# A vision tower's first stage: half-integer angles about the middle of each part, the lower half read backwards

## The chip, the core and the metric

The kernel runs on one core of one Trainium2 chip. The core has a matrix engine (PE, with PEld for its weight loads), a vector engine (VectorE, DVE), a scalar engine (ScalarE, ACT), GpSimd (POOL) and a queue of DMA issues (SyncE, SP). The metric is device time in microseconds, from the launch of the program to its end, taken as the median of several executions.

## The reference, cut to what is computed

The first stage makes an S4D convolution kernel for 64 images `c` and 128 rows `h`:

```
dtA = (-exp(inv_A_real) + 1j * A_imag) * exp(log_dt)[:, None]        # 128 x 64
Cc  = (C[..., 0] + 1j*C[..., 1]) * (B[..., 0] + 1j*B[..., 1]) * (exp(dtA) - 1) / A
V   = exp(dtA[:, :, None] * arange(1024))
h   = 2 * einsum('chn,hnl->chl', Cc, V).real                         # 64 x 128 x 1024
h   = h + attention(layernorm(h));  h = h + ffn_with_lora(layernorm(h))
```

The attention and the feed-forward part run over 64 sequences of 128 tokens of width 1024; the change doesn't touch them.

## The kernel before

The program has three blocks with a barrier of all engines between them: the token stage (`token_kernel`), the preparation of the weights (`prepare_weights`), and the tower (attention and feed-forward, `turns`). The token stage writes its result to `tok_h` in device memory, and the tower reads it back.

**Splitting the length.** The 1024 positions are cut into `L1` = 4 parts of `L0` = 256. A position is part times 256 plus an offset, and exp(dtA * position) is exp(dtA * 256 * part) times exp(dtA * offset). The first factor goes into tables per part (`gre`, `gim`, built from `wmag`, `wre`, `wim` and the sines in `whole`), the second is made anew for each row h: `v` holds exp(re * offset) times the sine of the angle. Partitions are the 64 states n times two: even partitions have a quarter turn added (`C_Q`), so they hold the cosine, odd ones the sine.

**Chunks.** 128 rows h are worked in `NCH` = 16 chunks of `CH` = 8. `tabc` holds one chunk's columns of the tables: part tables for `z`, the rate for the exponential, the turns per step for the angle (row `NT - 1`). For each chunk:

- VectorE copies `tabc` (L395), computes for each of 8 rows the whole number of turns `k` (L399, offset times turns plus the quarter, written as an integer), and for each of 8 the fraction `u` (L404); 256 columns each.
- ScalarE makes `v` = exp (L292, eight of 256 columns) and the sine of `u` (L298, one of 2048 columns), in the order of `decay` and `sine`, which change places in every chunk, so that each chunk has one load of a function table.
- VectorE multiplies `v` by `u` (L411, one of 2048 columns).
- PE turns the input into `ct1`, `ct2` (L454); VectorE multiplies them by the part tables into `z` and `z2` (L419, L420); GpSimd adds the two (L244) and swaps pairs of the input into `xs` (L231).
- PE multiplies `z` by `v` into `kps` (L472): per row h two products, q = 0 and q = 1, each for two of the four parts.
- ScalarE copies `kps` to `kout` (L283), which has two halves of four rows; SP stores each half with two DMAs, e = 0 and 1 (L204).
- VectorE takes one sixteenth of the maximum of the raw weights (`part_max`, L426).

**The order of the work** is written out by hand and the same in every chunk. VectorE's `body(ch)` is: `tabc`, `k`, `u` of chunk ch + 1; `v` of chunk ch; `z`, `z2` of chunk ch + 1; `part_max`. GpSimd's sum of chunk ch waits for `z_parts` of ch and for `v_ready` of ch. PE's `kps` of chunk ch waits for that sum and for `v`. VectorE's `z` of chunk ch + 1 waits until GpSimd's sum of ch - 1 and PE's `kps` of ch - 1 are done, since `z` has two buffers (L417, L418). ScalarE's exponentials of chunk ch + 1 wait for the same `kps` (L290). A copy to the first row of a `kout` half waits for the stores of the chunk before (L282). SP's `body(ch)` is: two loads of the input of chunk ch + 3 (behind a wait for PE's transposes), two loads of the weight `wo`, and four stores of chunk ch - 1.

**Where the parts stand.** `out_v` (L146) reads the 1024 positions as (q e l): q and e pick the part, e is the half of the partitions and of a DMA. So a DMA writes, for each c and h, two runs of 256 numbers, 1 KB each, with 1 KB between them.

Of the kernel before, what the change touches and what calls it, by code (L numbers as in the profile page):

```python
# [7 lines left out]
P = 128  # L8
ALU = mybir.AluOpType
# [33 lines left out]
C_ONE = C_OWN + 1  # L43
C_ALL = C_ONE + 1


def constants():
# [13 lines left out]
    c[:, C_OWN] = np.arange(P) // R  # L61
    c[:, C_ONE] = 1
    return c


def token_kernel(nc, sem, x, log_dt, b_re_im, inv_a, a_imag, const, ident, w, tok_h):
# [3 lines left out]
    with ExitStack() as ctx:  # L70
# [12 lines left out]
        re = sb("re", [P, NS])  # L83
        turns = sb("turns", [P, 8, NS])
        whole = sb("whole", [P, 8, NS])
        sines = whole
        e0 = sb("e0", [P, NS])
        th = sb("th", [P, NS])
        wmag = sb("wmag", [P, L1 - 1, NS])
        wre = sb("wre", [P, L1 - 1, NS])  # L90
        wim = sb("wim", [P, L1 - 1, NS])
        gre = sb("gre", [P, L1, NS])
# [9 lines left out]
        xs = sb("xs", [P, 2, CH // 2, NS, 2])  # L102
        u = sb("u", [P, 2, CH, L0])
        k = sb("k", [P, CH, L0], I32)
        qb = sb("qb", [P, 1])
# [4 lines left out]
        tmp = spare[:, 0, 0:18 * NS].rearrange("p (i n) -> p i n", n=NS)  # L110
        mix = spare[:, 1, 0:18 * NS].rearrange("p (i m n) -> p i m n", i=6, n=NS)
        part_max = sb("part_max", [P, NCH])

# [141 lines left out]
        def _(act):  # L255
            def step(ins):
                ins.then_inc(s_at, 1)
# [6 lines left out]
            step(nc.scalar.activation(th[:, :], re[:, :], ACT.Tanh, scale=0.5))  # L264
            for m in range(1, L1):
                step(nc.scalar.activation(wmag[:, m - 1], re[:, :], ACT.Exp, scale=float(m * L0)))
            act.wait_ge(s_dt, 12)
            step(nc.scalar.activation(sines[:, :, :], turns[:, :, :], ACT.Sin, scale=TURN))
# [44 lines left out]
        def _(dve):  # L313
# [15 lines left out]
            step(TS(turns[:, 1], turns[:, 0], 0.5, None, ALU.mult))  # L329
            for m in range(1, L1):  # L330
                step(TS(turns[:, 2 * m], turns[:, 0], float(m * L0), None, ALU.mult))
                step(TS(turns[:, 2 * m + 1], turns[:, 0], float(m * L0), 0.25, ALU.mult, ALU.add))
            step(TS(tab_c[:, 0, NT - 1], turns[:, 0], 1.0, None, ALU.mult))
            TS(whole[:, :, :], turns[:, :, :], ROUND, -ROUND, ALU.add, ALU.add).then_inc(s_whole, 1)
            dve.wait_ge(s_whole, 1)
            step(TT(turns[:, :, :], turns[:, :, :], whole[:, :, :], ALU.subtract))
            dve.wait_ge(s_at, 8)
            t = [tmp[:, i] for i in range(18)]
# [23 lines left out]
            step(STT(t[1], t[16], 2.0, bi, ALU.mult, ALU.mult))  # L362
            step(TT(gre[:, 0], t[0], t[1], ALU.add))
            step(STT(t[2], t[15], 2.0, bi, ALU.mult, ALU.mult))
            step(STT(t[3], t[16], 2.0, br, ALU.mult, ALU.mult))
            step(TT(gim[:, 0], t[2], t[3], ALU.subtract))

            sc = sines[:, 2:2 * L1].rearrange("p (m a) n -> p a m n", a=2)
            step(TT(wim[:, :], wmag[:, :], sc[:, 0], ALU.mult))
            step(TT(wre[:, :], wmag[:, :], sc[:, 1], ALU.mult))  # L370
            g0r = gre[:, 0:1].to_broadcast([P, L1 - 1, NS])
            g0i = gim[:, 0:1].to_broadcast([P, L1 - 1, NS])
            step(TT(mix[:, 0], g0r, wre[:, :], ALU.mult))
            step(TT(mix[:, 1], g0i, wim[:, :], ALU.mult))
            step(TT(gre[:, 1:L1], mix[:, 0], mix[:, 1], ALU.subtract))
            step(TT(mix[:, 2], g0r, wim[:, :], ALU.mult))
            step(TT(mix[:, 3], g0i, wre[:, :], ALU.mult))
            step(TT(gim[:, 1:L1], mix[:, 2], mix[:, 3], ALU.add))

# [9 lines left out]
            def body(ch, r):  # L389
                nxt = 1 - r  # L390
                if exists(ch + 1):
                    if exists(ch - 1):

                        dve.wait_ge(s_e, ch)
                    V.tensor_copy(tabc[:, nxt], tab[:, :, bass.ds((ch + 1) * CH, CH)]).then_inc(s_tabc, 1)  # L395
                    dve.wait_ge(s_tabc, ch + 2)

                    for h in range(CH):
                        ins = TS(k[:, h], const[:, C_L0:C_L0 + L0], tabc[:, nxt, NT - 1, h:h + 1],  # L399
                                 const[:, C_Q:C_Q + 1], ALU.mult, ALU.add)  # L400
# [1220 lines left out]
```

## Time and profile before

| | us |
|---|---|
| median of three runs | 3096.68 |
| lowest and highest | 3093.18, 3097.64 |
| the profiled execution, its own time | 3095.41 |
| its span, first to last instruction | 3093.6 |
| token stage, to the barrier behind it | 268.8 |
| preparation of the weights and start of the tower, to 362 | 93.2 |
| the rest of the tower | 2731.6 |

Over the whole span PE is busy 2852.0 us (92%), VectorE 2500.3, GpSimd 1966.9, ScalarE 1913.8. Times in rows of the trace count from the first instruction. In a row of the stretches of time each engine has its busy time and the number of its instructions; `PEclk` is the granted clock of the matrix engine as a share of 2.4 GHz. In a row of the timeline the first two numbers are start and length in us, and the bracket at the end holds the idle time before and what ended it; a row with x8 is eight instructions from the start of the first to the end of the last, which overlap a little.

### The profile page before, as it was taken

How to read it: one execution, taken by the hardware profiler on the slowest of the kernel's cores; microseconds unless marked ns; L12 is line 12 of the kernel's file. 1: busy time of each engine (PE TensorE's matmuls, PEld its weight loads, DVE VectorE, ACT ScalarE, POOL GpSimd, SP SyncE). 2: the span in 40 equal slices, each digit the busy share in tenths (PEclk: the TensorE clock that was granted, in tenths of full speed). 3: DMA queues.
4: the chain of work that ended last, by engine and by line, in shares of the span. 5: the costliest groups of instructions: out<-in, count | busy, mean ns of one | idle time of the engine just before them, and what ended most of it. 6: DMA issues, size and time to landing. Idle time of an engine off the chain costs nothing.

```text
span 3093.6 us, 62128 instructions
## 1 busy us (share of the span) xinstructions
PE 2852.0 (92%) x16986; PEld 1418.5 (46%) x16986; DVE 2500.3 (81%) x8865; ACT 1913.8 (62%) x5932; POOL 1966.9 (64%) x1722
## 2 busy tenths in 40 slices
PE   3767469999999999999999999999999999999986
PEld 2556234444444444444444444444444444444442
DVE  8996568888888888888888888888888888888872
ACT  5775356666666666666666666666666666666651
POOL 2441157667777767676777676777776776777762
PEclk9887789999999999999999999999999999999998
DMA  5887166676666666766666666666666666666751
GB/s 160 190 182 176 33 125 142 141 150 148 148 143 146 147 148 141 152 147 147 144 146 148 148 141 152 148 148 143 146 145 147 143 150 146 150 142 149 140 125 52
DMA packets 1269008, 442.53 MB, mean 143 GB/s; under 512 B 1200048, under 2 KB 1241264, under 8 KB 1268800
## 3 DMA queue, kind: packets, MB, share of 16 engines
q1 hardware_dynamic: 1268800, 440.62, 65.2%
q14 instruction: 183, 1.50, 0.2%
q8 instruction: 25, 0.41, 0.1%
HBM read 88.15 MB, written 67.11 MB: 50 GB/s over the span
## 4 chain that ended last, share of the span: by engine, by line
PE 38%; DVE 19%; issue 13%; POOL 10%; ACT 7%; DMA 1%; DVEq 0%; ACTq 0%; POOLq 0%; SPq 0%
PE bank_b L1437 18%; PE bank_a L1437 13%; DVE heads L1258 6%; DVE probs L1204 5%; ACT probs L1079 5%; POOL p_hl L1004 4%; POOL probs L1000 3%; PE bank_c L1437 3%; PE score L1408 2%; POOL rope_a L1010 2%; DVE share L1213 2%; POOL xy_hl L1019 1%; PE pv L1426 1%; DVE r L1286 1%; DVE zs L1366 1%
## 5 line engine op out<-in xcount | busy, mean ns | idle before, releaser
L1079 ACT ACTIVATE probs<-probs,negmax 128x128 f32<-128x128 f32 x2048 | 789.7, 387 | 268.9 <-DVE negmax L1204 268.9
L1004 POOL TENSOR_TENSOR p_hl<-probs,p_hl 128x512 f16<-128x512 f32 x512 | 614.9, 1201 | 354.6 <-ACT p_hl L1088 352.3
L1000 POOL TENSOR_TENSOR probs<-probs,rsum 128x512 f32<-128x512 f32 x512 | 556.7, 1087 | 221.7 <-DVE rsum L1215 220.1
L1437 PE MATMUL bank_a<-qkv_hi,xt 128*128 128x512 f16 x2048 | 655.7, 382 | 28.9 <-DMA xt<-xy_hl 28.9
L1204 DVE CUSTOM_DVE_ANT_0 probs<-score,table,scal 128x128 f32<-128x128 f32 x2048 | 596.5, 347 | 58.2 <-issue 56.9
L1437 PE MATMUL bank_b<-b_hi,yt 128*128 128x512 f16 x2048 | 643.1, 381 | 0.0
L1088 ACT ACTIVATE p_hl<-probs 128x512 f16<-128x512 f32 x512 | 319.8, 625 | 424.7 <-POOL probs L1000 417.2
L1258 DVE TENSOR_TENSOR heads<-rope_a,heads 128x512 f16<-128x512 f32 x320 | 402.4, 1273 | 36.5 <-ACT heads L1109 36.5
L1437 PE MATMUL bank_a<-qkv_lo,xt 128*128 128x512 f16 x1024 | 390.7, 381 | 0.0
L1437 PE MATMUL bank_b<-b_lo,yt 128*128 128x512 f16 x1024 | 390.0, 381 | 0.0
L1437 PE MATMUL bank_b<-o_lo,at_hi 128*128 128x512 f16 x1024 | 388.9, 380 | 0.0
L1437 PE MATMUL bank_b<-o_hi,at_hi 128*128 128x512 f16 x1024 | 388.8, 380 | 0.0
L1437 PE MATMUL bank_b<-o_hi,at_lo 128*128 128x512 f16 x1024 | 388.7, 380 | 0.0
L1079 ACT ACTIVATION_READ_ACCUMULATOR probs<-probs,negmax 128x1 f32 x2048 | 382.9, 187 | 0.0
L1109 ACT ACTIVATE heads<-rope_a 128x512 f16<-128x512 f32 x320 | 192.7, 621 | 246.8 <-POOL rope_a L1010 241.5
L1437 PE MATMUL bank_c<-qkv_hi,xt 128*128 128x512 f16 x1024 | 325.9, 380 | 0.0
L1437 PEld LDWEIGHTS bank_a<-qkv_hi,xt 128*128 128x128 f16 x2048 | 201.3, 98 | 271.7 <-issue 32.4
L1437 PEld LDWEIGHTS bank_b<-b_hi,yt 128*128 128x128 f16 x2048 | 201.0, 98 | 222.2 <-issue 4.6
L1019 POOL TENSOR_TENSOR xy_hl<-xyn,xy_hl 128x1024 f16<-128x1024 f32 x128 | 273.0, 2133 | 30.6 <-ACT xyn L1121 25.6
L1213 DVE TENSOR_TENSOR share<-sums,small 128x4 f32<-128x4 f32 x512 | 198.3, 387 | 72.0 <-ACT probs L1079 53.0
L1010 POOL TENSOR_TENSOR rope_a<-rope_a,rope_b 128x512 f32<-128x512 f32 (+1 forms) x192 | 208.9, 1088 | 36.8 <-DVE rope_b L1241 34.0
L1408 PE MATMUL score<-kstack,stack 128*128 128x128 f16 x2048 | 198.5, 220 | 24.9 <-DVE negmax L1204 17.9
(199 smaller groups left out, 4525.2 us busy)
## 6 DMA issues: line engine op xcount, KB each, us to landing
tok_h<-kout SPq DMA_DIRECT2D x64, 512.0 KB, 5.9
hin<-tok_h SPq DMA_DIRECT2D x64, 512.0 KB, 3.3
r<-tok_h SPq DMA_DIRECT2D x64, 512.0 KB, 3.5
out_dram<-r SPq DMA_DIRECT2D x64, 512.0 KB, 2.9
probs_t<-p_hl SPq DMA_TRANSPOSE x512, 2.8
xc<-in_x_dram SPq DMA_DIRECT2D x32, 128.0 KB, 4.7
raw_a<-in_L_attn_wq_dram SPq DMA_DIRECT2D x1, 4096.0 KB, 14.4
raw_b<-in_L_attn_wo_dram SPq DMA_DIRECT2D x32, 128.0 KB, 3.8
```

Of the source, the lines that this page charges most:

```text
L1000: TT(x, x, rsum[:, u % 4].unsqueeze(2).to_broadcast([P, GR, T]), ALU.mult).then_inc(s_norm, 1)
L1004: TT(p_hl[:, u % 2, 1], probs[:, u % 4], p_hl[:, u % 2, 0], ALU.subtract).then_inc(s_plo, 1)
L1010: TT(rope_a[:, 0:hs], rope_a[:, 0:hs], rope_b[:, 0:hs], ALU.add).then_inc(s_rope2, 1)
L1019: TT(xy_hl[:, 1], xyn[:, :], xy_hl[:, 0], ALU.subtract).then_inc(done, 1)
L1079: ins = A(probs[:, u % 4, g], probs[:, u % 4, g], ACT.Exp, bias=negmax[:, u % 4, g:g + 1], scale=-1.0, accum_out=sums[:, u % 4, g:g + 1])
L1088: A(p_hl[:, u % 2, 0], probs[:, u % 4], ACT.Copy).then_inc(s_phi, 1)
L1109: A(dst, src, ACT.Copy).then_inc(s_hhi, 1)
L1204: ins = V.tensor_tensor_reduce(probs[:, u % 4, g], score[u % 2][:, g], mask, col(U_SC), 3e38, ALU.add, ALU.min, negmax[:, u % 4, g:g + 1])
L1213: TT(share[:, u % 4], sums[:, u % 4], small[:, :], ALU.mult).then_inc(s_share, 1)
L1258: TT(dst, full_.unsqueeze(2).to_broadcast([P, 8, 2, HD]), hi, ALU.subtract).then_inc(s_hlo, 1)
L1408: ins = MM(score[u % 2][:, g], stack[:, h // 8, h % 8], kstack[:, par, u], start=True, stop=True)
L1437: ins = MM(bank, x(c), w[:, c, cols], start=(c == 0 and i == 0), stop=(c == KC - 1 and i == 2))
```

## The change

The offset inside a part is taken about the middle of the part. The part tables now belong to the position 256 * part + 127.5, for all four parts (before, part 0 had no factor of its own); so there are four pairs of sines instead of three, and `wmag`, `wre`, `wim` have four rows. The offsets of a part are then -127.5 to 127.5, and the angle of a negative offset is that of the positive one with the sign turned. `k`, `u` and the sine are made for the 128 positive half-integer offsets alone. The cosine is even and the sine odd: the upper half of `v` is multiplied by `u` as it stands, the lower half by `u` read backwards (a step of -1) times `C_SIGN`, +1 on even partitions and -1 on odd ones. The exponential is still taken for 256 columns, from offset 0 on; its part factor remains that of the start of the part.

`PART` = (0, 2, 1, 3) gives the order of the parts in the tables, and `out_v` reads the positions as (e q l). The products q = 0 and q = 1 of one half of the partitions are now neighbouring parts, and a DMA writes one run of 512 numbers, 2 KB, for each c and h.

```diff
+PART = (0, 2, 1, 3)
+LH = L0 // 2
...
+    c[0::2, C_SIGN] = 1
+    c[1::2, C_SIGN] = -1
+    c[:, C_HALF:C_HALF + L0 // 2] = np.arange(L0 // 2)[None, :] + 0.5
...
-        u = sb("u", [P, 2, CH, L0])
-        k = sb("k", [P, CH, L0], I32)
+        u = sb("u", [P, 2, CH, LH])
+        k = sb("k", [P, CH, LH], I32)
...
-        out_v = tok_h.rearrange("c h (q e l) -> e c h q l", e=2, l=L0)
+        out_v = tok_h.rearrange("c h (e q l) -> e c h q l", e=2, l=L0)
...
-            for m in range(1, L1):
-                step(nc.scalar.activation(wmag[:, m - 1], re[:, :], ACT.Exp, scale=float(m * L0)))
+            for i in range(L1):
+                step(nc.scalar.activation(wmag[:, i], re[:, :], ACT.Exp, scale=float(PART[i] * L0)))
...
-            for m in range(1, L1):
-                step(TS(turns[:, 2 * m], turns[:, 0], float(m * L0), None, ALU.mult))
-                step(TS(turns[:, 2 * m + 1], turns[:, 0], float(m * L0), 0.25, ALU.mult, ALU.add))
+            for i in range(L1):
+                middle = PART[i] * L0 + LH - 0.5
+                step(TS(turns[:, 2 * i + 2], turns[:, 0], middle, None, ALU.mult))
+                step(TS(turns[:, 2 * i + 3], turns[:, 0], middle, 0.25, ALU.mult, ALU.add))
...
-                        ins = TS(k[:, h], const[:, C_L0:C_L0 + L0], tabc[:, nxt, NT - 1, h:h + 1],
+                        ins = TS(k[:, h], const[:, C_HALF:C_HALF + LH], tabc[:, nxt, NT - 1, h:h + 1],
...
-                        ins = STT(u[:, nxt, h], const[:, C_L0:C_L0 + L0], tabc[:, nxt, NT - 1, h:h + 1], k[:, h],
+                        ins = STT(u[:, nxt, h], const[:, C_HALF:C_HALF + LH], tabc[:, nxt, NT - 1, h:h + 1], k[:, h],
...
-                    TT(v[:, r], v[:, r], u[:, r], ALU.mult).then_inc(s_v, 1)
+                    upper, lower = v[:, r, :, LH:L0], v[:, r, :, 0:LH]
+                    TT(upper, upper, u[:, r], ALU.mult)
+                    STT(lower, u[:, r, :, ::-1], const[:, C_SIGN:C_SIGN + 1], lower, ALU.mult, ALU.mult).then_inc(s_v, 1)
```

The remaining lines of the diff widen the tables: `turns` and `whole` from 8 to 10 rows, the products of the table step from 192 to 256 columns, the result for the first position in a place of its own (`g0`), and the constants by 129 columns.

On VectorE, one chunk near the start of the program (its `tabc` to its `part_max`), first in the kernel before:

```order
L395 COPY tabc<-tab 128x80
L399 TENSOR_SCALAR k<-const,tabc 128x256 x8
L404 SCALAR_TENSOR_TENSOR u<-const,tabc,k 128x256 x8
L411 TENSOR_TENSOR v<-v,u 128x2048
L419 TENSOR_TENSOR z<-ct,tabc 128x2048
L420 TENSOR_TENSOR z<-ct,tabc 128x2048
L426 TENSOR_REDUCE part_max<-raw_a 128x1
```

and the same chunk on VectorE in the changed kernel:

```order
L404 COPY tabc<-tab 128x80
L408 TENSOR_SCALAR k<-const,tabc 128x128 x8
L413 SCALAR_TENSOR_TENSOR u<-const,tabc,k 128x128 x8
L421 TENSOR_TENSOR v<-v,u 128x8x128
L422 SCALAR_TENSOR_TENSOR v<-u,const,v 128x8x128
L430 TENSOR_TENSOR z<-ct,tabc 128x2048
L431 TENSOR_TENSOR z<-ct,tabc 128x2048
L437 TENSOR_REDUCE part_max<-raw_a 128x1
```

Nothing changes its place; `k` and `u` have half their columns, and the one product for `v` became two, of which the second releases GpSimd and PE.

On GpSimd, the sums and swaps of the first chunks of the changed kernel, which stand as before:

```order
L239 TENSOR_TENSOR xs<-xc,const 128x256 x6
L252 TENSOR_TENSOR z<-z 128x2048
L239 TENSOR_TENSOR xs<-xc,const 128x256 x2
L252 TENSOR_TENSOR z<-z 128x2048
L239 TENSOR_TENSOR xs<-xc,const 128x256 x2
```

The sum of `z` still stands right behind the wait for `v`, with one swap of the input between two sums.

## Rows read from the trace of the kernel before

**Rows 1.** Stretches of time: length, then busy time of each engine.

```profile
43.39:239.64 196.25, 133.53 (x543) 110.90 (x544) 191.59 (x296) 151.54 (x248) 78.39 (x40) 0.88 0.76 172
239.64:268.78 29.14, 18.42 (x75) 14.68 (x73) 10.95 (x8) 17.39 (x30) 9.43 (x4) 0.92 0.82 193
```

The engines stand in the order PE, PEld, DVE, ACT, POOL; behind them the granted clock, the DMA share and GB/s.

**Rows 2.** Groups of VectorE between 43.3 and 239.6 us: busy us, mean ns.

```profile
L404 DVE SCALAR_TENSOR_TENSOR u<-const,tabc,k 128x256 f32<-128x256 f32 x113 | 46.1, 479 | 0.5
L399 DVE TENSOR_SCALAR k<-const,tabc 128x256 int32<-128x256 f32 x112 | 38.7, 417 | 0.5
...
L411 DVE TENSOR_TENSOR v<-v,u 128x2048 f32<-128x2048 f32 x14 | 32.0, 2284 | 0.0
```

**Rows 3.** Waits between 43 and 248 us: total, times, longest.

```profile
DVE z L419 <- PE kps L472: 3.6, 4, 1.4
```

**Rows 4.** Timeline, chunks 0 to 2 and the `v` of chunk 14.

```profile
43.39 2.28 DVE L411 TENSOR_TENSOR v<-v,u 128x2048 f32<-128x2048 f32 x1
45.59 2.28 DVE L419 TENSOR_TENSOR z<-ct,tabc 128x2048 f32<-128x2048 f32 x1
45.82 4.52 POOL L244 TENSOR_TENSOR z<-z 128x2048 f32<-128x2048 f32 x1 [12.38 <-DVE v L411]
...
50.39 9.93 PE L472 MATMUL kps<-v,z 128*128 128x256 f32 x32 [10.95 <-POOL z L244]
...
57.13 2.28 DVE L411 TENSOR_TENSOR v<-v,u 128x2048 f32<-128x2048 f32 x1
...
60.46 2.29 DVE L419 TENSOR_TENSOR z<-ct,tabc 128x2048 f32<-128x2048 f32 x1 [1.05 <-PE kps L472]
...
65.45 2.00 ACT L298 ACTIVATE u<-u,qb 128x2048 f32<-128x2048 f32 x1
...
65.95 2.67 DVE L399 TENSOR_SCALAR k<-const,tabc 128x256 int32<-128x256 f32 x8
68.66 3.26 DVE L404 SCALAR_TENSOR_TENSOR u<-const,tabc,k 128x256 f32<-128x256 f32 x8
71.84 2.28 DVE L411 TENSOR_TENSOR v<-v,u 128x2048 f32<-128x2048 f32 x1
...
239.64 2.28 DVE L411 TENSOR_TENSOR v<-v,u 128x2048 f32<-128x2048 f32 x1
```

**Rows 5.** PE's `kps`: timeline of chunks 1 and 2, stretches of chunks 1 and 10.

```profile
64.14 7.57 PE L472 MATMUL kps<-v,z 128*128 128x256 f32 x32 [2.95 <-POOL z L244]
...
78.93 5.44 PE L472 MATMUL kps<-v,z 128*128 128x256 f32 x14 [6.34 <-POOL z L244]
...
191.29 7.08 PE L472 MATMUL kps<-v,z 128*128 128x256 f32 x21 [6.34 <-POOL z L244]
...
64.14:71.71 7.57, 7.44 (x34) 6.21 (x35) 7.50 (x19) 5.23 (x7) 1.09 (x2) 1.00 0.90 224
191.29:200.75 9.46, 9.46 (x34) 7.95 (x35) 8.87 (x19) 5.77 (x11) 1.41 (x3) 0.75 0.76 161
```

**Rows 6.** Groups of VectorE before 26 us, the table step.

```profile
L332 DVE TENSOR_SCALAR turns<-turns 128x64 f32<-128x64 f32 x3 | 0.6, 195 | 0.1
L341 DVE SCALAR_TENSOR_TENSOR z<-whole 128x64 f32<-128x64 f32 x1 | 0.2, 226 | 0.8 <-ACT whole L268 0.8
...
L361 DVE SCALAR_TENSOR_TENSOR z<-z,bri x1: 226/226/226, 15.9 to 15.9; 128x64 f32<-128x64 f32 x1
```

**Rows 7.** Timeline of ScalarE's last copies, behind the fifteenth `v`.

```profile
259.98 2.06 ACT L283 ACTIVATE kout<-kps 128x512 f32<-128x512 f32 x4 [3.85 <-DMA tok_h<-kout]
264.21 2.07 ACT L283 ACTIVATE kout<-kps 128x512 f32<-128x512 f32 x4 [2.16 <-DMA tok_h<-kout]
```

**Rows 8.** One instruction's ns (least, median, most), and two stretches of time.

```profile
L1258 DVE TENSOR_TENSOR heads<-rope_a,heads x320: 661/853/2859, 372.8 to 2989.9; 128x512 f16<-128x512 f32 x160
...
10.00:20.00 10.00, 0.00 (x0) 0.00 (x0) 8.23 (x31) 0.63 (x1) 0.86 (x1) 1.00 1.02 412
131.00:134.00 3.00, 0.00 (x0) 0.00 (x0) 3.00 (x2) 2.97 (x6) 3.00 (x1) 1.00 0.93 221
```

More of the change, by code:

```diff
@@ L43 @@
 C_ONE = C_OWN + 1
-C_ALL = C_ONE + 1
+C_SIGN = C_ONE + 1
+C_HALF = C_SIGN + 1
+C_ALL = C_HALF + L0 // 2
 def constants():
@@ L83, in token_kernel @@
         re = sb("re", [P, NS])
-        turns = sb("turns", [P, 8, NS])
-        whole = sb("whole", [P, 8, NS])
+        turns = sb("turns", [P, 2 + 2 * L1, NS])
+        whole = sb("whole", [P, 2 + 2 * L1, NS])
         sines = whole
@@ L88, in token_kernel @@
         th = sb("th", [P, NS])
-        wmag = sb("wmag", [P, L1 - 1, NS])
-        wre = sb("wre", [P, L1 - 1, NS])
-        wim = sb("wim", [P, L1 - 1, NS])
+        wmag = sb("wmag", [P, L1, NS])
+        wre = sb("wre", [P, L1, NS])
+        wim = sb("wim", [P, L1, NS])
+        g0 = sb("g0", [P, 2, NS])
         gre = sb("gre", [P, L1, NS])
@@ L110, in token_kernel @@
         tmp = spare[:, 0, 0:18 * NS].rearrange("p (i n) -> p i n", n=NS)
-        mix = spare[:, 1, 0:18 * NS].rearrange("p (i m n) -> p i m n", i=6, n=NS)
+        mix = spare[:, 1, 0:6 * L1 * NS].rearrange("p (i m n) -> p i m n", i=6, n=NS)
         part_max = sb("part_max", [P, NCH])
@@ L264, in _ @@
             step(nc.scalar.activation(th[:, :], re[:, :], ACT.Tanh, scale=0.5))
-            for m in range(1, L1):
-                step(nc.scalar.activation(wmag[:, m - 1], re[:, :], ACT.Exp, scale=float(m * L0)))
-            act.wait_ge(s_dt, 12)
+            for i in range(L1):
+                step(nc.scalar.activation(wmag[:, i], re[:, :], ACT.Exp, scale=float(PART[i] * L0)))
+            act.wait_ge(s_dt, 14)
             step(nc.scalar.activation(sines[:, :, :], turns[:, :, :], ACT.Sin, scale=TURN))
@@ L336, in _ @@
             step(TT(turns[:, :, :], turns[:, :, :], whole[:, :, :], ALU.subtract))
-            dve.wait_ge(s_at, 8)
+            dve.wait_ge(s_at, 9)
             t = [tmp[:, i] for i in range(18)]
@@ L362, in _ @@
             step(STT(t[1], t[16], 2.0, bi, ALU.mult, ALU.mult))
-            step(TT(gre[:, 0], t[0], t[1], ALU.add))
+            step(TT(g0[:, 0], t[0], t[1], ALU.add))
             step(STT(t[2], t[15], 2.0, bi, ALU.mult, ALU.mult))
             step(STT(t[3], t[16], 2.0, br, ALU.mult, ALU.mult))
-            step(TT(gim[:, 0], t[2], t[3], ALU.subtract))
-            sc = sines[:, 2:2 * L1].rearrange("p (m a) n -> p a m n", a=2)
+            step(TT(g0[:, 1], t[2], t[3], ALU.subtract))
+            sc = sines[:, 2:2 * L1 + 2].rearrange("p (m a) n -> p a m n", a=2)
             step(TT(wim[:, :], wmag[:, :], sc[:, 0], ALU.mult))
             step(TT(wre[:, :], wmag[:, :], sc[:, 1], ALU.mult))
-            g0r = gre[:, 0:1].to_broadcast([P, L1 - 1, NS])
-            g0i = gim[:, 0:1].to_broadcast([P, L1 - 1, NS])
+            g0r = g0[:, 0:1].to_broadcast([P, L1, NS])
+            g0i = g0[:, 1:2].to_broadcast([P, L1, NS])
             step(TT(mix[:, 0], g0r, wre[:, :], ALU.mult))
             step(TT(mix[:, 1], g0i, wim[:, :], ALU.mult))
-            step(TT(gre[:, 1:L1], mix[:, 0], mix[:, 1], ALU.subtract))
+            step(TT(gre[:, :], mix[:, 0], mix[:, 1], ALU.subtract))
             step(TT(mix[:, 2], g0r, wim[:, :], ALU.mult))
             step(TT(mix[:, 3], g0i, wre[:, :], ALU.mult))
-            step(TT(gim[:, 1:L1], mix[:, 2], mix[:, 3], ALU.add))
+            step(TT(gim[:, :], mix[:, 2], mix[:, 3], ALU.add))
             step(V.tensor_copy(tab_c[:, 0, 0:L1], gre[:, :]))
```

## The prediction

> **What bounds the kernel now.** The first look is at where the changed stage lies. By the stretches of time, the first stage with its sixteen chunks ends at 268.78 us; between the first `v` product (43.39 us) and the fifteenth (239.64 us) VectorE is busy 191.6 of 196.25 us, PE 133.5, ScalarE 151.5, GpSimd 78.4 [rows 1]. Read by that alone, the stage is VectorE's, and every VectorE microsecond taken away comes back. The groups of instructions say how it is spent: per chunk 8 instructions for `k`, 8 for `u`, one for `v`, two for `z`, one for `part_max` [rows 2].
>
> The waits say something finer. VectorE's own waits are only 3.6 us, but all of them are its `z` product waiting for PE's `kps` [rows 3]. That wait closes a loop over two chunks: the `v` product of chunk c releases GpSimd's sum of `z`; that releases the `kps` matmuls of chunk c; their end frees the `z` buffer for chunk c+2; behind that, on VectorE, stand `z`, `z2`, `part_max`, `tabc`, `k` and `u` of chunk c+2, and then a `v`. From the rows of chunk 0: `v` starts at 43.39, GpSimd at 45.82 (2.43 later), PE at 50.39 (4.57), `z` at 60.46 (PE 9.93 and 0.14 more), the `v` of chunk 2 at 71.84 (11.38). The sum is 28.45 us for two chunks: with no slack anywhere [rows 4]. Over the seven such pairs the mean is (239.64 - 43.39)/7 = 28.04 us [rows 4]. VectorE alone, without the wait, takes 13.74 us from the `v` of chunk 0 to that of chunk 1 [rows 4], 27.5 us a pair. So loop and engine lie 2% apart, and the question is what each loses.
>
> **The change part by part.**
>
> `k` and `u`, 128 instead of 256 columns, 8 of each a chunk. 2048 columns of `v` take 2284 ns and the next instruction starts 2.20 us after it; 64 columns take 226 ns [rows 2, 4, 6]: (2284 - 226)/1984 = 1.04 ns a column. So each of the 16 loses 128 x 1.04 = 0.133 us. `k` to `u` is 2.71 us now (65.95 to 68.66), `u` to `v` 3.18 us [rows 4]; they become 1.64 and 2.11. **2.13 us less a chunk.**
>
> `v`, one product of 2048 columns, becomes a product of 1024 columns and a second instruction of 1024 columns that reads `u` backwards. The columns are the same in number. The extra start is 2.20 - 2048 x 1.04 = 0.07 us [rows 2, 4]; instructions of the second kind cost some more to start (`u`: 479 ns for 256 columns, against 417 for `k` [rows 2]), 0.06 us. **0.13 us more a chunk**, on VectorE as well as in the loop, if the backward read costs what a forward one does. No row shows a backward read. From below, nothing excludes a saving but nothing can give one either, for both forms already run at one column each 1.04 ns. From above, the slowest two-input product of this kernel is the `heads` one, 2859 ns for 512 columns beside 661 at best [rows 8], that is 5.6 ns a column: 4.6 us more a chunk. The nearest row is a strided read: `bri` is read with a step of two, and takes 226 ns for 64 columns, as do the products of the same size with step one [rows 6]. I take no extra cost, and keep the upper end for a rival.
>
> The Trainium skill speaks against this. "Vector Engine (DVE) Microarchitecture Reference", section 5.2 on the measured stream behaviour, says that a port runs at its full rate only where successive elements come as adjacent pairs of words, and gives 1.73 ns a column where one source hops at every element; it adds that a negative step was not measured. By that figure the estimate is 0.7 us more for a chunk's backward half. The step-two read above does not bear the rule out, since 64 columns would be 0.04 us slower by it.
>
> `Sin` on 1024 instead of 2048 columns takes about 1 us off ScalarE. ScalarE is busy 151.5 us in 196.25 [rows 1] and is not what the loop passes through. Behind the end of chunk 0's `kps` (60.32) its copy, the exponentials, a table load and the sine of chunk 2 are through at 67.45, 7.1 us later [rows 4]; that becomes 6.1, while the `v` that needs them follows `kps` by 0.14 + 9.25. So nothing is won there, and some 3 us of cover are left.
>
> **The loop after.** v to GpSimd 2.43 + 0.12, GpSimd to PE 4.57, PE as now, `z` to `v` 11.38 - 2.13. The loop holds only one chunk's worth of `k` and `u` for its two chunks, so it loses 2.0 us, not the 4.0 that VectorE loses: 28.04 - 2.0 = 26.0 us a pair. VectorE alone would need 2 x (13.74 - 2.0) = 23.5. The `z` wait takes the place of what was removed: about 2.5 us a pair, all of it before every second chunk, since the odd chunk follows the even one at VectorE's pace, 11.7 us later. Seven pairs: **14.0 us less** between the two `v`.
>
> PE's term rests on its clock. `kps` took 7.57 us at a granted clock of 1.00 (2.4 GHz) behind an idle stretch of 2.95 us, and 9.46 us with a granted clock of 0.75 on average (part at 1.2 GHz) behind one of 6.34 us [rows 5]. In the new schedule the odd chunk's `kps` starts 11.7 us after the even one's, PE stands idle about 1.5 us (11.7 less 9.3 and 0.9 of transposes, 71.71 to 72.59 [rows 5]) and should stay at 2.4 GHz; but that chunk's loop has slack. The even chunk's starts 14.3 us after the odd one's, which takes 7.6, and the transposes 0.9: idle 5.8 us, so it should start at 1.2 GHz as it does now. The loop that decides keeps its slow PE.
>
> **Before the first `v`.** `k` and `u` of chunks 0 and 1 lose 2 x 2.13 = 4.3 us. The tables grow: two more steps of 0.2, eight products of 256 instead of 192 columns (8 x 64 x 1.04 = 0.53 us), the two over 640 instead of 512 columns and the sine of the same size 0.13 each [rows 6], and 66 KB more of constants before the first step, 0.2 to 0.3 us at 412 to 221 GB/s [rows 8], if nothing hides it. Together 1.5 us more. **2.8 us less.**
>
> **Behind the fifteenth `v`.** 29.1 us now [rows 1]. `kps` of chunk 14 follows as before. The last copies wait for stores: 3.85 and 2.16 us [rows 7]. The stores' runs become 2 KB. Loads in 4 KB runs moved 412 GB/s at a full DMA share, the mix with stores in 1 KB runs 221 GB/s at 0.93 [rows 8]. A store pair of 1 MB that took 4.2 us (259.98 to 264.21 [rows 7]) then takes 3.3 or so. Two pairs: 1.7 us less, between 0 and 3.5. Between the two `v` no copy waits for a store, so the longer runs win nothing there.
>
> **The sum:** 14.0 + 2.8 + 1.7 = 18.5 us less. What follows the stage starts at its end and depends on nothing that has an earlier fixed time, so it moves as a whole. The profiled execution is 3095.41 us, 3093.6 of them span; it lies 1.3 us under the median of three, 3096.68. From it 3076.9; from the median 3078.2. I give 3077.5.
>
> **The rivals.**
>
> *PE keeps 2.4 GHz in both chunks.* Then `kps` takes 7.6 instead of 9.3 us in the deciding loop, 1.7 a pair, 12 us in all: 3065. For it: gaps of 2.95 us kept the clock. Against: the gap before even chunks should be 5.8. Chance 0.12.
>
> *The stage is VectorE's after all,* because PE's wait disappears in some way that I don't see: seven pairs of 23.5, 32 + 4.5 us less: 3060. The loop above adds up to 0.01 us, so 0.03.
>
> *The backward read runs at half speed,* 1.07 us more for each of 15 chunks. Both `v` and VectorE carry it, but the even loop holds it once a pair, so 7 or 8 times 1.07: 8 to 9 us of the gain are gone, 3086. This is the rival that the skill's rule of adjacent pairs gives, at its price somewhat less. Chance 0.15.
>
> *Slower than before:* the backward read costs so much that it eats everything. 18.5 us over 8 is 2.3 us a chunk, 3.3 ns a column; from there on it is slower. At the 5.6 ns of the slowest product, 4.6 us a chunk, VectorE takes over with 2 x (11.7 + 4.6) = 32.6 a pair, 4.6 more than now, and once more behind the fifteenth: 3095.4 + 32 + 5 - 4.5 = 3128. Chance 0.04. That the half-size instructions hit a floor and save nothing is the same to the reader and nearly excluded: 64 columns run in 195 to 226 ns.
>
> **How the numbers follow.** The forecast has 0.66, and its own range is 3072 to 3083 (table cost, tail 0 to 3.5 us, PE's term up to 0.5 us a pair either way). The range goes down to the clock rival and up to the slow read: 3063 to 3088. About 0.2% (6 us) is what a measurement of this kernel can tell from no change; only a backward read at 2.5 to 4 ns a column ends there, which I take out of the slow read's chance. Faster 0.91, same 0.05, slower 0.04.
>
> **What would show it.** In the profile after: `k` near 280 ns and `u` near 345 ns; the second `v` instruction near 1.28 us (a slow read shows there, at once); the wait of `z` for `kps` grown from 3.6 us to 15 or 20 us; `v` starts alternating at 11.7 and 14.3 us; PE's granted clock falling only before even chunks; ScalarE's two waits for `kout` stores near the end shortened. It is wrong if ScalarE's `v` exponentials or the stores' landing become a wait before `v` or `kps`.

## The result and the profile after

| us | before | after |
|---|---|---|
| median, lowest and highest | 3096.47 (3093.18 to 3097.64) | 3116.56 (3115.38 to 3118.36) |
| the profiled execution, its span | 3095.41, 3093.6 | 3116.39, 3114.6 |
| first `v` product | 43.39 | 40.86 |
| `v` product of chunk 14 | 239.64 | 230.88 |
| end of the token stage | 268.78 | 258.93 |
| tower's first scores on VectorE | 389.10 | 381.30 |
| tower's last scores on VectorE | 3022.7 | 3043.6 |

The changed kernel is slower: the ratio is 1.0066, with an interval of 1.005 to 1.0082. I had forecast 3077.5 and given "slower" a chance of 0.04. One execution below, of the kernel without GpSimd's wait, took 3496.0 us at a granted clock of 0.83 instead of 0.96, and no ratio counts it. The table splits the miss in two. The token stage gained 9.9 us where 18.5 were forecast, and the tower, in which no line of code was changed, lost 28.7 (the preparation between them took 2.1 more).

The stretches of time, columns as in [rows 1]; first the stage (against [rows 1]), then preparation and tower of after:

```profile
40.86:230.88 190.02, 133.13 (x550) 109.84 (x551) 170.23 (x310) 138.16 (x248) 78.44 (x40) 0.89 0.77 179
230.88:258.93 28.05, 16.35 (x67) 13.21 (x66) 11.13 (x10) 16.58 (x30) 9.43 (x4) 0.86 0.83 198
258.93:381.30 122.37, 71.87 (x348) 53.13 (x348) 74.62 (x119) 47.82 (x71) 10.66 (x14) 0.71 0.33 81
381.30:3043.60 2662.30, 2581.62 (x15752) 1216.02 (x15753) 2176.79 (x8312) 1673.96 (x5538) 1849.06 (x1644) 0.99 0.67 143
```

The same stretches of before, which the earlier sections didn't need:

```profile
268.78:389.10 120.32, 70.37 (x348) 52.70 (x348) 74.60 (x119) 48.17 (x72) 10.66 (x14) 0.71 0.33 83
389.10:3022.70 2633.60, 2578.53 (x15752) 1214.73 (x15753) 2175.11 (x8312) 1673.26 (x5538) 1849.94 (x1644) 0.99 0.67 145
```

In the tower each engine runs the same instructions, PE at the same clock, and each is busy as long as before to 3.1 us. So the 28.7 us are idle time. VectorE's waits between 700 and 2700 us that end on "issue" (in total, times, longest), of before:

```profile
DVE probs L1204 <- issue: 25.7, 51, 0.7
DVE share L1213 <- issue: 13.2, 24, 0.9
```

and of after, where `L1215` is the old `L1204`:

```profile
DVE stats L1272 <- issue: 38.9, 24, 2.1
DVE probs L1215 <- issue: 17.1, 24, 0.7
```

24 times, once in each pass of VectorE's loop in this stretch, VectorE stands still for 1.6 us ahead of `stats`, and no semaphore holds it: "issue" is time for which the profile shows no wait. PE feels it a little later. Its waits in the same stretch grow from 14.9 us to 36.7 in all; before, and then after:

```profile
PE pv L1541 <- DVE zs L1366: 14.9, 24, 1.1
```

```profile
PE pv L1552 <- DVE zs L1377: 28.7, 24, 1.2
PE pv L1437 <- DMA probs_t<-p_hl: 6.6, 11, 1.0
PE pv L1437 <- issue: 1.4, 8, 0.3
```

The place is just behind the loop's jump. One pass on the timeline of VectorE, before. The jump is no row: in the program it stands between the first two rows, and VectorE's sequencer takes it at 796.93, while the engine still works off what was issued ahead of it:

```profile
797.97 0.74 DVE L1293 SCALAR_TENSOR_TENSOR r<-bank_c,scal,r 128x512 f32<-128x512 f32 x1
799.85 0.75 DVE L1278 SCALAR_TENSOR_TENSOR r<-bank_b,scal,r 128x512 f32<-128x512 f32 x1 [1.14 <-PE bank_b L1437]
800.64 0.69 DVE L1261 BATCH_NORM_STATS2 stats<-r 128x6 f32<-128x512 f32 x1
```

and after (the jump at 792.42):

```profile
793.46 0.74 DVE L1304 SCALAR_TENSOR_TENSOR r<-bank_c,scal,r 128x512 f32<-128x512 f32 x1
795.43 0.75 DVE L1289 SCALAR_TENSOR_TENSOR r<-bank_b,scal,r 128x512 f32<-128x512 f32 x1 [1.23 <-PE bank_b L1448]
797.98 0.69 DVE L1272 BATCH_NORM_STATS2 stats<-r 128x6 f32<-128x512 f32 x1 [1.80 <-issue]
```

Each kernel stops once at the jump. The bracket names PE, but by the records of VectorE's sequencer the first instruction behind the jump comes 2.8 us after it before and 2.9 after, and the product follows 0.14 us later. After has a second stop one product further on. A pass of two sequences takes 82.44 us before and 83.54 after (median of 27); 28 passes by 1.1 us are 31.

The stops go with the arrival of code. The page of after has this row (packets, MB, share) among its DMA queues:

```profile
q14 instruction: 183, 1.50, 0.2%
```

1.50 MB in 183 packets are 8.2 KB each. Five of them come back in every pass: by the records of the packets they start 1.0, 3.6, 6.7, 32.5 and 61.6 us behind the jump before, and 1.0, 3.5, 6.6, 33.7 and 59.4 after (medians over the passes). So the body of the loop is fetched anew in every pass. That VectorE waits for it behind the jump is read from these times: in the pass shown of after, the first two loads have landed 1.75 and 4.2 us behind the jump, and the two stops end at 2.9 and 5.6. In the compiled program VectorE's loop has 379 instructions. In front of it stand 954 before and 964 after: two more steps of the tables, and the second `v` instruction, written out in eight places. By the figures of the Trainium skill, "Runtime: NRT & Kernel Launch", section "Instruction fetch mechanics", 256 instructions are 16 KiB, 64 bytes each, and 16 KiB is a block. The loads of this queue are half as large, and the measurement decides: by 64 bytes each, one holds 128 instructions. The place of the loop's start in such a block moves from 58 to 68 (954 and 964 less whole 128s). It is counted as if a block began with the program's first instruction; that isn't shown, and only the distance between two kernels, modulo 128, is used here. The same section warns that a taken branch whose target isn't loaded stalls the engine until it is; the rows here agree. That the place matters, not only the jump, had to be tried.

### The profile page after: what moved, and what is told of

Same layout as the page of the kernel before. It is cut to its first block, busy times and chain, and to the rows that moved or that the text cites. A ratio compares the mean times of both kernels' runs of the same rounds, so it can differ in the third digit from the quotient of the medians.

```text
span 3114.6 us, 62147 instructions
## 1 busy us (share of the span) xinstructions
PE 2854.2 (92%) x16986; PEld 1417.7 (46%) x16986; DVE 2478.4 (80%) x8883; ACT 1899.3 (61%) x5933; POOL 1966.1 (63%) x1722
## 4 chain that ended last, share of the span: by engine, by line
PE 39%; DVE 18%; issue 13%; POOL 10%; ACT 7%; DMA 2%; DVEq 0%; ACTq 0%; POOLq 0%; SPq 0%
PE bank_b L1448 20%; PE bank_a L1448 12%; DVE heads L1269 6%; DVE probs L1215 5%; ACT probs L1090 5%; POOL p_hl L1015 4%; POOL probs L1011 3%; PE bank_c L1448 2%; PE score L1419 2%; DVE share L1224 2%; POOL rope_a L1021 1%; PE pv L1437 1%; POOL xy_hl L1030 1%; DVE r L1297 1%; DVE zs L1377 1%
## 5 line engine op out<-in xcount | busy, mean ns | idle before, releaser
L1215 DVE CUSTOM_DVE_ANT_0 probs<-score,table,scal 128x128 f32<-128x128 f32 x2048 | 598.7, 348 | 50.0 <-issue 49.3
L1024 POOL TENSOR_TENSOR rstd<-var,minus_half 128x1 f32<-128x1 f32 x128 | 70.8, 553 | 264.4 <-DVE var L1281 231.5
```

The costliest lines, as they stand in the source:

```text
L1024: TT(rstd[:, :], var[:, :], minus_half[:, :], ALU.pow).then_inc(done, 1)
L1215: ins = V.tensor_tensor_reduce(probs[:, u % 4, g], score[u % 2][:, g], mask, col(U_SC), 3e38, ALU.add, ALU.min, negmax[:, u % 4, g:g + 1])
```

## The experiments

Eleven more kernels ran, in three sets: the first four below, the next four, and the last three, of which the kernel before without its loop is one. Each is compared with the kernel before as run beside its set (medians 3100.72, 3095.74 and 3099.62). In the first set, theory C says that the place of VectorE's code makes the loss, and its rival that the wider constants do, which move the tiles behind them in memory.

**Ten idle instructions in the kernel before.** Behind the last chunk VectorE waits for the barrier; there it now fills ten single columns of a tile that nobody reads.

```diff
+        fill = sb("fill", [P, 128])
...
             V.tensor_reduce(w["mx"][:, 0:1], part_max[:, :], AX_X, ALU.max).then_inc(w["s_mx"], 1)
+            for i in range(10):
+                V.memset(fill[:, i:i + 1], 0.0)
```

> The kernel before, with 10 one-column fills more on VectorE where it stands idle for 17 us at the end of the first stage. 10 is the number of VectorE instructions by which the change makes the program longer ahead of the tower's loop. Theory C (the code's place): in the changed kernel VectorE stands still twice behind the loop's jump, once for 1.8 us where nothing else is due, since the loop's first instructions lie otherwise in the blocks in which code is loaded; so these 10 idle fills alone cost what the change cost in the tower, 25 to 30 us, and the kernel takes 3120 to 3127. Theory M (memory): the tower is slower since constants or the stored result lie otherwise in memory; then 10 fills cost nothing, 3096.

Measured: 3129.54 us, a ratio of 1.0094 (1.0077 to 1.0111). The fills themselves cost 0.19 us inside an idle stretch, by VectorE's timeline:

```profile
250.51 0.19 DVE L435 MEMSET fill<- 128x1 f32 x10
268.38 0.15 DVE L639 TENSOR_SCALAR mxa<-mxa 128x1 f32<-128x1 f32 x1 [17.68 <-PEq L70]
```

The stretch of the tower and VectorE's wait in it are those of after:

```profile
388.70:3055.70 2667.00, 2581.72 (x15752) 1216.02 (x15753) 2176.06 (x8312) 1673.73 (x5538) 1849.73 (x1644) 0.99 0.67 143
```

```profile
DVE stats L1264 <- issue: 42.8, 24, 2.1
```

So ten instructions that do nothing, ahead of the tower, cost 29 us. The kernel before, without one line of the change in it, shows the whole loss. The new tile `fill` isn't the cause: the kernels with 118 and with 16 fills below have the same tile, and their towers take 2634.8 and 2647.5 us.

**The wider constants alone.**

```diff
-C_ALL = C_ONE + 1
+C_ALL = C_ONE + 1 + 129
```

> The kernel before with the 129 further columns of constants and nothing else: every tile and every array in device memory behind it moves as in the changed kernel, VectorE's code stays. Theory M: 3115 to 3125. Theory C: 3096 to 3097 (0.2 us for the longer load).

Measured: 3099.27 us, 0.9997 (0.9988 to 1.0007). The rival falls.

**The changed kernel with 118 fills**, so that 10 + 118 = 128 instructions stand ahead and the loop has its old place in a block.

```diff
+            for i in range(118):
+                V.memset(fill[:, i:i + 1], 0.0)
```

> The changed kernel with 118 fills more on VectorE in its 16.6 us of idle time before the barrier: with the 10 of the change a whole block of 128 instructions (8 KB), so the tower's loop lies in its block as in the kernel before. Theory C: the 29 us of the tower come back, and what is left is the first stage's gain of 9.9 us less some 2 us of the weights' preparation: 3086 to 3090. Theory M: 3116.

Measured: 3089.05 us, 0.9958 (0.9941 to 0.9975). The second stop is gone, and PE's wait has its old length:

```profile
383.10:3017.90 2634.80, 2580.00 (x15752) 1214.52 (x15753) 2175.46 (x8312) 1673.72 (x5538) 1849.93 (x1644) 0.99 0.67 145
```

```profile
PE pv L1555 <- DVE zs L1380: 15.6, 24, 1.2
```

Pushing the loop to the same place brings the tower back to 2634.8 us against 2633.6, and what the change is worth by itself comes out: 11.7 us by the medians, 0.4%, with an interval of some 8 to 18 us. The traces say less: the two profiled executions differ by 4.6 us (3095.41 and 3090.78). The change also lengthens ScalarE's code by one instruction ahead of its loop. That is still so here, so it costs nothing that shows.

**Sixteen fills** put the loop's start at 84 in its block.

```diff
+            for i in range(16):
+                V.memset(fill[:, i:i + 1], 0.0)
```

> The changed kernel with 16 fills more: the block's edge, which now lies some 8 instructions behind the loop's entry, comes to lie before it. Theory C: one stall a pass instead of two; 3080 to 3092, unless the edge falls on another wait. Theory M: 3116.

Measured: 3101.54 us, 1.0005 (0.9995 to 1.0014), above what I expected. There is one stop again, but a longer one, up to 2.7 us:

```profile
DVE r L1292 <- issue: 51.9, 24, 2.7
```

The loads come 0.5, 1.0 and 4.3 us behind the jump here. I had taken one stop as good as another, and had put the edge of a block some 8 instructions behind the loop's entry, where the count above has 60. That the place costs something in three sizes is shown (table below); a rule that gives the size from the place I don't have.

**Stores in runs of 1 KB again**, with the 118 fills.

```diff
-PART = (0, 2, 1, 3)
+PART = (0, 1, 2, 3)
...
-        out_v = tok_h.rearrange("c h (e q l) -> e c h q l", e=2, l=L0)
+        out_v = tok_h.rearrange("c h (q e l) -> e c h q l", e=2, l=L0)
```

> The changed kernel with 118 fills, and with the order of the parts and of the stores as before (two runs of 1 KB instead of one of 2 KB). Against the same with 2 KB runs (3089.0). Theory of the prediction: the longer runs are worth only the last copies' waits for stores; those were 3.85 and 2.16 us and are 3.29 and 1.77 in the changed kernel, so this is 0.5 to 2 us slower, 3089.5 to 3091, and the wait behind the fifteenth v grows by that. Rival (the stores' landing became a wait in the faster stage, or the tower gains from the order of the parts): 5 us or more slower.

Measured: 3085.93 us, 0.9971 (0.996 to 0.9982), where I had expected 3089.5 to 3091; the interval overlaps that of the 2 KB runs (0.9941 to 0.9975). ScalarE's waits for the stores behind chunk 14, with 1 KB and then with 2 KB:

```profile
ACT kout L292 <- DMA tok_h<-kout: 5.7, 2, 3.6
```

```profile
ACT kout L292 <- DMA tok_h<-kout: 5.0, 2, 3.3
```

So the longer runs are worth 0.7 us of waiting in these two traces, less than the times can tell.

**GpSimd's sum no longer waits for `v`**, 118 fills. If the loop of two chunks is what sets the pace, cutting its first link should speed it up.

```diff
-                    pool.wait_ge(s_v, ch + 1)
```

> The changed kernel with 118 fills, where GpSimd's sum of z no longer waits for v (it doesn't read v; PE waits for both anyway). Theory L (the loop through GpSimd and PE is what holds the stage): v releases PE directly, the loop of two chunks loses some 4.6 us, VectorE's wait for kps (18.8 us in the changed kernel) vanishes, and a pair of chunks goes from 27.15 to 24.5 us: 17 to 19 us less, 3070 to 3073. Rival P (the sum now runs beside VectorE's own reads): GpSimd's 4.5 us fall on part_max, k and u; u, which reads two tiles, takes up to twice as long, and a part or all of the gain is gone: 3075 to 3095, u's mean well over 345 ns.

Measured: 3126.68 us, 1.0098 (1.0078 to 1.0118), worse than either account had it; a pair of chunks takes 32.5 us (mean of the first seven), where the kernel with 118 fills has 27.3. GpSimd starts right behind `z2`, and VectorE's copy of `tabc` runs into it. From the timeline in the middle of the stage:

```profile
151.53 4.53 POOL L252 TENSOR_TENSOR z<-z 128x2048 f32<-128x2048 f32 x1 [10.65 <-DVE z L431]
152.22 3.90 DVE L404 COPY tabc<-tab 128x80 f32 x1
```

The copy takes 0.19 us in after and 3.9 here, and ends when the sum does (156.06 and 156.12). `part_max` (0.95 us) runs beside the sum unharmed. Two copies a pair at 3.7 us more, on top of VectorE's own 24.6 (twice the 12.28 us from one `v` to the next, where it doesn't wait), would make 32.0: nearly the whole pair. So the wait that I took for a mere link of the loop also keeps GpSimd away from the copy.

**The loop away.** Now VectorE's loop of the tower is changed, and that of no other engine; 118 fills with the first edit, none with the others.

```diff
-        def turns(eng, turn):
+        def turns(eng, turn, step=2):
...
-            with eng.Fori(2, CB // 2 - 2) as pair:
-                turn(pair * 2, 0, True, True, True, True, True)
-                turn(pair * 2 + 1, 1, True, True, True, True, True)
+            if step:
+                with eng.Fori(4 // step, (CB - 4) // step) as some_:
+                    for i in range(step):
+                        turn(some_ * step + i if i else some_ * step, i % 2, True, True, True, True, True)
+            else:
+                for b in range(4, CB - 4):
+                    at(turn, b)
...
-            turns(dve, turn)
+            turns(dve, turn, 4)
```

> The changed kernel with 118 fills, and VectorE's loop of the tower written out for four turns a pass instead of two (same work, 14 jumps instead of 28; the other engines keep their loops). Theory C: a jump costs 1.4 us of standstill that shows, and the delay behind it; half of them gone is 14 x 1.4 to 14 x 2 us: 3061 to 3070. If the standstill has cover elsewhere: 3085 to 3090.

Measured with four sequences in a pass, half as many jumps: 3075.61 us, 0.9938 (0.9921 to 0.9954). And with VectorE's part written out, in the changed kernel and in the kernel before, by the same edit with another last line:

```diff
-            turns(dve, turn)
+            turns(dve, turn, 0)
```

> The changed kernel without fills, VectorE's part of the tower written out wholly, so that it has no jump there and its code comes in order. Theory C: no standstill behind a jump, and the place of the code doesn't matter any more: 28 x 1.4 to 28 x 2 us less than 3089, 3033 to 3050. Rival: code that is never used twice has to be loaded all along (about 80 blocks more), and the loads become waits of their own: 3070 or more.

> The kernel before with VectorE's part of the tower written out wholly, no loop, as in a_flat. Between this and a_flat nothing is left of the code's place, so the pair gives what the change is worth by itself. Theory C: a_flat less the first stage's 9.9 us: the profiled executions differ by 8 to 11 us, this one at 3073 to 3078 where a_flat has 3065 to 3067; the runs' ratio to the kernel before is near 0.993 (a_flat: 0.990). If the change slows the tower in another way too, the two come out alike.

Measured: 3065.29 us, 0.9898 (0.9881 to 0.9915), for the changed kernel, and 3072.57 us, 0.9916 (0.9899 to 0.9932), for the kernel before. The tower of the former:

```profile
383.00:2994.00 2611.00, 2573.94 (x15752) 1217.29 (x15753) 2142.04 (x8314) 1673.48 (x5538) 1848.75 (x1644) 0.99 0.66 146
```

So in the kernel before the loop costs 23 us of the tower and 27 of the whole, 0.8%. I had expected more (3061 to 3070 with four sequences a pass, 3033 to 3050 written out): a jump costs 0.9 us of the tower in both (2634.8 less 2621.7 over 14 jumps, 2634.8 less 2610.9 over 28), not the 1.4 to 2 that I took. The packets bear out whose code it is: the queue `q14` has 155 of them with four sequences a pass and 115 with VectorE's part written out. Between the two kernels without a loop the ratios differ by 0.0018, 5.6 us, and the profiled executions by 5.1 (3072.14 and 3067.03), below the 8 to 11 that I had expected; the intervals of the two ratios overlap.

With its part written out, VectorE is also busy some 33 us less in the tower (2142 against 2175), which I didn't follow up.

All towers in one table, sorted by the place of the loop's start in a block of 128 (counted as above); the time is from the first to the last scores on VectorE, read from each trace:

| place | tower, us |
|---|---|
| 58 | before 2633.6, wider constants 2637.3, 118 fills 2634.8, 1 KB runs 2633.2, GpSimd without its wait 2634.2 |
| 68 | after 2662.3, ten fills 2667.0 |
| 84 | sixteen fills 2647.5 |
| four sequences a pass | 2621.7 |
| no loop | 2610.9, 2610.6 (before), 2610.0, 2609.1 |

Inside a row the traces agree within 5 us, from row to row they differ by at least 10.

**`tabc` and `k` in other forms**, loop written out. The copy becomes a product with a column of ones, `k` an instruction with two tile inputs, to see whether it is the copy's form that runs into GpSimd.

```diff
-                    V.tensor_copy(tabc[:, nxt], tab[:, :, bass.ds((ch + 1) * CH, CH)]).then_inc(s_tabc, 1)
+                    TT(tabc[:, nxt], tab[:, :, bass.ds((ch + 1) * CH, CH)],
+                       const[:, C_ONE:C_ONE + 1].unsqueeze(1).to_broadcast([P, NT, CH]), ALU.mult).then_inc(s_tabc, 1)
...
-                        ins = TS(k[:, h], const[:, C_HALF:C_HALF + LH], tabc[:, nxt, NT - 1, h:h + 1],
-                                 const[:, C_Q:C_Q + 1], ALU.mult, ALU.add)
+                        ins = STT(k[:, h], const[:, C_HALF:C_HALF + LH], tabc[:, nxt, NT - 1, h:h + 1],
+                                  const[:, C_Q:C_Q + 1].to_broadcast([P, LH]), ALU.mult, ALU.add)
```

> a_flat, with two VectorE instructions of the first stage in another form, the results the same: tabc by a product with a column of ones instead of a copy, k by the form with two tile inputs (u's form). Reason: k lost only 0.52 ns a column when it was halved (407 to 340 ns), u 1.04, so k and the copy read one tile through two ports. Theory R (that form needs the port that GpSimd uses, and waits for GpSimd): k rises or falls by under 10 ns in the middle, but its 520 ns maxima and tabc's 0.56 and 0.66 us ones beside GpSimd's swap are gone; the stage is held by the loop, so its length changes by under 2 us.

Measured: 3063.67 us (3063.17 to 3065.05), 0.9886 (0.9869 to 0.9902). That can't be told from the kernel without this edit (0.9898), but lies 8.9 us under the kernel before without its loop, which ran beside it (3072.14 to 3074.42). It is the fastest kernel here. The long instructions that I had expected to vanish are still there: `k` reaches 585 ns (520 before the edit) and `tabc` 540.

The same with GpSimd's wait taken out:

```diff
-                    pool.wait_ge(s_v, ch + 1)
```

> a_oneport, and GpSimd's sum doesn't wait for v, as in a_free. In a_free the copy of tabc took 3.89 instead of 0.2 us, since it waited for GpSimd's sum to end, and the pair of chunks rose to 32.7 us. Theory R: with no instruction in the two-port form between z2 and v, the sum of GpSimd runs beside part_max, tabc, k and u, and only VectorE's own time is left: a pair near 2 x 12.2 = 24.5 us, the stage 17 to 19 us shorter than in a_flat, 3045 to 3050. Theory P (any VectorE instruction with two tile inputs loses beside GpSimd): k and u rise, to as much as twice, a pair stays at 27 us or more, 3065 or more.

Measured: 3105.07 us, 1.0018 (1.0009 to 1.0028), a pair 32.8 us. The account that only the copy's form collides falls: the product stands still as long as the copy did. `k` and `u` keep their medians (339 and 346 ns), since the sum is over when they start.

```profile
152.91 4.52 POOL L251 TENSOR_TENSOR z<-z 128x2048 f32<-128x2048 f32 x1 [10.76 <-DVE z L431]
153.60 3.93 DVE L403 TENSOR_TENSOR tabc<-tab,const 128x80 f32<-128x80 f32 x1
```

The Trainium skill, "SBUF — State Buffer", section "Who interferes with whom", lists both: a copy in its fast mode and any VectorE instruction with two inputs in SBUF block against a GpSimd instruction that reads SBUF. The rows agree. `z` and `z2`, with one input in PSUM, keep their 2.28 us beside the sum.

## Why the prediction was wrong

**The step that failed** is the sentence under the sum: "What follows the stage starts at its end and depends on nothing that has an earlier fixed time, so it moves as a whole." It is true of the data and of the semaphores, and for those I had looked. It isn't true of the code: ten instructions more on VectorE shift everything behind them in the program, and a loop that is fetched anew in each of 28 passes meets that shift 28 times. Shown by the kernel before with ten fills (+29 us) and the changed kernel with 118 (the loss gone). The chance for "slower" had the wrong mechanism too: it put the loss into the backward read. There were rows to be looked at: [rows 1] ends with the first stage, and no group holds VectorE's waits of the tower, where "issue" ends 24 waits of `share`, one in each pass. Such a wait, once a pass, is a mark of the loop.

**The stage, term by term.** Of 18.5 us it gave 9.85 in the profiled pair. Over the four traces with the stage of before its end lies between 266.3 and 268.8, over five with the changed stage between 258.9 and 260.9; the means differ by 7.6. The groups of after that answer to [rows 2] (least, median, most ns of one):

```profile
L408 DVE TENSOR_SCALAR k<-const,tabc x128: 332/340/520, 27.7 to 228.4; 128x128 int32<-128x128 f32 x128
L413 DVE SCALAR_TENSOR_TENSOR u<-const,tabc,k x128: 342/345/352, 29.8 to 230.6; 128x128 f32<-128x128 f32 x128
L421 DVE TENSOR_TENSOR v<-v,u x16: 1214/1217/1227, 40.9 to 238.7; 128x1024 f32<-128x1024 f32 x16
L422 DVE SCALAR_TENSOR_TENSOR v<-u,const,v x16: 1275/1279/1283, 42.0 to 239.9; 128x1024 f32<-128x1024 f32 x16
```

- *Backward read:* right. 1279 ns for 1024 columns, forecast 1.28 us; a forward product of the same size takes 1217, and 60 of the 62 ns between them were forecast for the form. That the 60 fit is luck: they were `u` less `k` at 256 columns, and `k` runs at half the price a column (next point). At 128 columns the two differ by 5 ns. The price that I had taken from the rule of adjacent pairs, 0.7 us more a chunk, isn't there, and the rival built on it is gone. The columns of a backward read are neighbours too, so the rule itself isn't tested by it.
- *`u`:* right, 345 ns as forecast.
- *`k`:* wrong by half. From 407 to 340 ns for 128 columns less is 0.52 ns a column, where I took 1.04 from the two-input products. `k` has one tile input and another form; its own rate wasn't in the rows that I used, since all `k` were of one size. The Trainium skill has a reason for it: by "VectorE: DVE Perf Modes", section "Mode 2×_2P", an instruction with a single tile input, in SBUF, reads it through both ports, two numbers at a time, and one with two tile inputs can't. The measured slopes agree; no run changed the number of tile inputs at 256 columns. Worth 8 x 128 x 0.52 = 0.53 us a chunk, 3.7 in the seven pairs.
- *The loop:* its form was right, its length wasn't. `z` waits for `kps` 18.8 us in all (forecast 15 to 20, against [rows 3]), and the `v` starts alternate at 12.3 and 14.9 us (forecast 11.7 and 14.3). The wait, then one loop from chunk 4 to chunk 6 on the timeline, against [rows 4]:

```profile
DVE z L430 <- PE kps L483: 18.8, 7, 2.8
```

```profile
94.64 1.22 DVE L421 TENSOR_TENSOR v<-v,u 128x1024 f32<-128x1024 f32 x1
...
97.20 4.52 POOL L252 TENSOR_TENSOR z<-z 128x2048 f32<-128x2048 f32 x1 [9.11 <-DVE v L422]
...
101.85 10.05 PE L483 MATMUL kps<-v,z 128*128 128x256 f32 x32 [5.72 <-POOL z L252]
...
106.92 1.21 DVE L421 TENSOR_TENSOR v<-v,u 128x1024 f32<-128x1024 f32 x1
...
112.04 2.29 DVE L430 TENSOR_TENSOR z<-ct,tabc 128x2048 f32<-128x2048 f32 x1 [2.71 <-PE kps L483]
...
121.82 1.22 DVE L421 TENSOR_TENSOR v<-v,u 128x1024 f32<-128x1024 f32 x1
```

  2.56 + 4.65 + 10.05 + 0.14 + 9.78 = 27.18 us; the mean of the seven is 27.15, forecast 26.0, before 28.04.
- *PE's term:* mis-sized. The even chunks' `kps` take 10.05 us on average over the seven pairs, before 9.34; I had let them stay. That is 0.71 us a pair, 5 us in all. With `k` it makes 26.0 + 0.53 + 0.71 = 27.24, against the 27.15 measured. The stretches of one even and one odd `kps` of after, against [rows 5]:

```profile
101.86:111.90 10.04, 10.04 (x34) 8.35 (x35) 7.39 (x20) 4.79 (x9) 3.46 (x3) 0.71 0.66 134
114.00:122.00 8.00, 7.00 (x31) 5.90 (x32) 7.93 (x21) 6.16 (x12) 1.14 (x2) 1.00 0.94 241
```

  Before, three even chunks, 4, 8 and 12:

```profile
106.86:115.71 8.85, 8.85 (x34) 7.43 (x35) 8.78 (x19) 5.77 (x11) 1.04 (x2) 0.81 0.85 172
162.49:172.69 10.20, 10.20 (x34) 8.43 (x35) 8.88 (x19) 5.78 (x12) 2.15 (x3) 0.70 0.74 150
219.26:228.12 8.86, 8.86 (x34) 7.48 (x35) 8.79 (x19) 5.76 (x12) 1.13 (x2) 0.81 0.73 147
```

  and on PE's timeline one even chunk of before; then one of after, with the odd one behind it (its first half of 16):

```profile
106.86 8.86 PE L472 MATMUL kps<-v,z 128*128 128x256 f32 x32 [4.46 <-POOL z L244]
```

```profile
129.03 10.12 PE L483 MATMUL kps<-v,z 128*128 128x256 f32 x32 [5.71 <-POOL z L252]
...
141.31 3.72 PE L483 MATMUL kps<-v,z 128*128 128x256 f32 x16 [1.29 <-POOL z L252]
```

  PE's idle stretches came out as forecast, 5.7 us (5.8) ahead of even and 1.2 to 1.7 us (1.5) ahead of odd chunks. The granted clock is 0.71 on average in the one and 1.00 in the other, so the rival that PE keeps its clock in both is out. What failed is the price. Before, three of the six even chunks behind the first had 0.81 and took 8.8 to 8.9 us, and three had 0.70 to 0.76 and took 9.3 to 10.2; after, all six have 0.70 to 0.72 and take 9.9 to 10.2. The mean that I kept was that of the mixture. The length of the idle stretch alone doesn't decide it: before, chunks 2 and 10 stood behind 6.34 us, longer than any of the six of after, and took 9.3 and 9.5, while chunk 8 stood behind 4.48 and took 10.2. Why the new rhythm gives every even chunk the long form stays open; no run changed PE's idle time alone.
- *Before the first `v`:* 2.53 us, forecast 2.8.
- *Behind the fifteenth:* 1.09 us (29.14 to 28.05), forecast 1.7. ScalarE's two waits for the stores went from 3.85 + 2.16 [rows 7] to 5.1 us. The kernel with runs of 1 KB (5.7 against 5.0 us, above) gives the longer runs 0.7 of that, which the times can't tell from nothing.

```profile
ACT kout L291 <- DMA tok_h<-kout: 5.1, 2, 3.3
```

Preparation and start of the tower took 122.4 us, before 120.3. Over all traces here it is 119.3 to 122.4, with the change and without, so I read nothing from it.

The signs of the steps were right, then, and their sum about twice too large: the price of `k` (3.7 us) and PE's term (5.0) account for the 8.7 that are missing. Neither decided the case. With the loop back in its place the changed kernel is faster than before by some 5 to 12 us, 0.2 to 0.4%, by whichever pair of kernels one takes, and the stage's own 7.6 lies in that; what the prediction left out, 29 us, is more than twice the most of it.

## What to carry to other kernels

Where an engine runs a loop, an edit anywhere ahead of it in that engine's code can move the time, by 1% here, without a semaphore or an instruction that explains it: count the instructions that an edit adds ahead of each loop, look for "issue" waits that come once a pass, and compare two versions only with the loop at the same place, or written out. Where the bound is a loop over several engines, ask what each of its links does when it is given more idle time, and take a column's price from the same instruction form, not from the nearest size. And before a wait is taken away, look at what would run beside what it holds back.

## What the runs showed of the hardware

- VectorE's loop of 379 instructions is fetched anew in each pass, in loads of 8.2 KB, five a pass. At the places 58 and 68 VectorE's sequencer has its first instruction 2.8 to 2.9 us behind the jump, partly beside work that is still running, and at 68 the engine stops for 1.6 us more; at 84 the first comes after 0.6 us, and one stop of 2.2 us (51.9 over 24) follows. Written out, the same work is 23 us shorter. "Issue" waits remain, and more of them (87.4 us in the changed kernel written out, 38.9 in the kernel before with its loop), but none longer than 0.9 us, and the list of PE's waits between 700 and 2700 us is empty: not their sum counts but whether one is long enough to reach PE.
- A read with a step of -1 runs at the rate of a forward one: 1279 ns for 1024 columns of fp32, against 1217 for a forward product; the same form (`u`) takes 345 ns for 128 columns and 479 for 256, so it costs 1.05 ns a column and has a larger start.
- `TENSOR_SCALAR` from fp32 to int32 with both scalars from a tile takes 0.52 ns more a column, half of what a two-input product takes (1.04).
- A copy of 80 columns took 3.90 us instead of 0.19, and a product of that size 3.93 instead of 0.23, beside a GpSimd sum of 2048 columns; both end with it.
